# Shared expert ahead of the output projection, and the denominators' inverse ahead of clips, ranks and softplus chain

## The reference

```python
mod = (_silu(c) @ wmod).reshape(8, 6, 1, -1)             # sa, ca, ga, sb, cb, gb; |ga|, |gb| kept >= 0.25
h = _layernorm(x) * (1 + ca) + sa
x = x + ga * attention(h, W_in, W_out)
h = _layernorm(x) * (1 + cb) + sb
x = x + gb * ffn(h, ...)
# attention: xq, xk = clip(q/4), clip(k/4); Chebyshev polynomials Tq, Tk of orders 0..5 (orders above have weight 0)
num = (Tq * beta * cumsum(Tk * v)).sum(order)            # running sums over the tokens
den = (Tq.sum(channel) * beta * cumsum(Tk.sum(channel))).sum(order)
out = (num / (den + 1e-7)) @ W_out.T
# ffn: one shared expert and 8 routed ones, hidden size 128, top 2 of sqrt(softplus(logits))
shared = silu(h @ sW1 + sb1) @ sW2 + sb2
routed = sum_e cf[:, e] * (silu(h @ rW1[e] + rb1[e]) @ rW2[e] + rb2[e])
```

## Time and profile before

| | |
|---|---|
| median of 3 runs | 915.92 us (915.1 to 918.37) |
| the profiled execution's own time | 915.11 us |
| its span | 913.4 us |
| TensorE busy | 847.7 us (93%) |
| VectorE busy | 798.7 us (87%) |
| ScalarE busy | 486.2 us (53%) |
| GpSimd busy | 275.1 us (30%) |
| mean granted TensorE clock | 0.968 of full speed |

### The profile page before, as it was taken

One profiled execution on the slowest core, in us unless ns is written; L12 is line 12 of the kernel. 1 busy time (PEld: TensorE's weight loads), 2 busy tenths in 40 slices (PEclk: granted clock), 3 DMA queues, 4 the chain that ended last, 5 costly groups with the idle time before them and its releaser, 6 DMA issues. The chain is left out here.

```text
span 913.4 us, 14235 instructions
## 1 busy us (share of the span) xinstructions
PE 847.7 (93%) x4377; PEld 645.8 (71%) x4377; DVE 798.7 (87%) x1363; ACT 486.2 (53%) x874; POOL 275.1 (30%) x351
## 2 busy tenths in 40 slices
PE   5784749999999999999999999999999999998998
PEld 5553437786868677886768676877768676866786
DVE  3897969999999989999899989999999999999432
ACT  4753446555656466565656466565656464441321
POOL 1021241423434241423333251523333240413120
PEclk9886859999999999999999999999999999999999
DMA  9022225354544435354534435363635344353431
GB/s 322 2 55 75 47 49 168 71 169 87 152 87 114 129 75 167 70 168 88 149 88 119 125 72 167 71 176 85 167 72 137 76 81 135 78 152 76 122 94 45
DMA packets 51580, 99.98 MB, mean 109 GB/s; under 512 B 5363, under 2 KB 34110, under 8 KB 49478
## 3 DMA queue, kind: packets, MB, share of 16 engines
q1 hardware_dynamic: 36356, 66.14, 22.0%
q0 software_dynamic: 14688, 32.51, 20.5%
q10 hardware_dynamic: 482, 0.74, 0.2%
HBM read 57.68 MB, written 17.06 MB: 82 GB/s over the span
## 5 line engine op out<-in xcount | busy, mean ns | idle before, releaser
L1577 PE MATMUL acc<-w,hid 128*128 128x256 f32 x1128 | 262.6, 380 | 0.3 <-DVE hid L1219 0.3
L1577 PEld LDWEIGHTS acc<-w,hid 128*128 128x128 f32 x1128 | 214.0, 190 | 34.5 <-DVE hid L1219 0.5
L848 ACT ACTIVATE hid<-ring,b1row 128x512 f32<-128x512 f32 x144 | 96.8, 682 | 165.9 <-PE ring L1458 164.5
L673 POOL DMA_DIRECT2D feat<-feat x47 | 42.6, 906 | 344.0 <-DVE feat L1066 210.4
L796 ACT ACTIVATE feat<-ring,bqkv 128x512 f32<-128x512 f32 x96 | 65.9, 687 | 87.4 <-PE ring L1458 87.4
L1219 DVE TENSOR_TENSOR hid<-hid,cfw 128x512 f32<-128x512 f32 x128 | 85.0, 675 | 29.3 <-ACT hid L848 22.0
L1458 PE MATMUL ring<-n2H,w1H 128*128 128x512 f32 x288 | 106.2, 450 | 0.0
L1045 DVE TENSOR_TENSOR_SCAN feat<-zero,carry,feat 128x512 f32<-128x512 f32 x80 | 97.2, 1267 | 0.0
L1045 DVE TENSOR_TENSOR_SCAN feat<-zero,feat 128x512 f32<-128x512 f32 x80 | 92.4, 1205 | 0.0
L1458 PE MATMUL ring<-n2H,w1L 128*128 128x512 f32 x288 | 91.0, 397 | 0.0
L1458 PE MATMUL ring<-n2L,w1H 128*128 128x512 f32 x288 | 91.0, 397 | 0.0
(11 more groups left out here) (169 smaller groups left out, 1397.9 us busy)
## 6 DMA issues: line engine op xcount, KB each, us to landing
feat<-feat POOLq DMA_DIRECT2D x47, 512.0 KB, 4.6
cfw<-cf_rows SPq DMA_DIRECT2D x16, 1280.0 KB, 7.6
xin<-in_L_attn_x SPq DMA_DIRECT2D x16, 512.0 KB, 9.5
feat<-inv_rows SPq DMA_DIRECT2D x32, 256.0 KB
cfw<-cf_rows SPq DMA_DIRECT2D x16, 512.0 KB, 3.6
out<-x SPq DMA_DIRECT2D x15, 512.0 KB, 8.6
out<-fin POOLq DMA_DIRECT2D x15, 512.0 KB, 5.8
cfw<-cf_rows SPq DMA_DIRECT2D x16, 256.0 KB, 4.6
```

What stands on the lines that cost most here:

```text
L673: g.dma_start(f(into), f(of), accum_op=ALU.add).then_inc(added[n], 16)
L848: a.activation(hid[:, e % NG], ring[bank][:, :], ACT.Silu, bias=b1row[:, e:e + 1]).then_inc(ring_copied, 1)
L1577: last = mm(acc[t // 2][:, t % 2], hid[:, e % NG, t * P:(t + 1) * P], w2[:, e], start=False, stop=(e == E), skip_group_check=True)
```

## The change

The work is the same but for two places of memory and one wait; its order changes on TensorE, VectorE and ScalarE. SyncE's and GpSimd's instructions stand in the same order as before.

1. TensorE: `begin`, new, stands ahead of `project_out`. It does for the chunk c-1 the first part of its expert work: `expert_up` of experts 0 and 1 and `expert_down` of expert 0, and then `combine_by_expert`, which stood behind `project_out`. The next step starts with expert 2. `expert_down` of expert 0 now starts the accumulators and waits until `output` of the chunk before has read them; `second_biases` adds to them.
2. TensorE, inside the step: the projections k0 and k1 stand ahead of the second norm's transposes, the experts' downs come later against the ups, and the sixth up and the fourth down stand behind `denominators` and no more ahead of it.
3. VectorE: the next chunk's second pair of `odd` and its first `weigh` stand behind `output` and ahead of `residual`, instead of behind the norm's `lows`; `lows` of the second norm stand behind the weighings of experts 1 and 2.
4. VectorE: `logit_parts` is cut in two. The maxima stay; the ranks (three instructions) go behind the denominators' products, and `invert` follows them directly, ahead of the clips, the weighing of expert 5 and `softplus`. The ranks' temporary is no more the tile `prod` but a part of `feat`.
5. ScalarE: the silus of experts 0 and 1 stand at a step's end, and expert 3's ahead of the second norm; the k copies ahead of `highs` of the second norm.
6. The steps at both ends follow: step 1, which has no expert work before, now holds `begin` for chunk 0; `last_attention_step`, `step_after_attention` and `last_step` are written out.

```diff
-        RING = ["e0", "e1", "e2", "k0", "k1", "q0", "q1", "e3", "e4", "e5", "v0", "v1", "e6", "e7", "e8"]
+        RING = ["e2", "e3", "k0", "k1", "q0", "q1", "e4", "e5", "v0", "v1", "e6", "e7", "e8", "e0", "e1"]
...
-                pool.wait_ge(squares, 6 * c + 6)
+                pool.wait_ge(weighted, (ND - 1) * c + 1)
                 g.tensor_tensor(f(W + 4), f(KT5), f(V0), ALU.mult).then_inc(weighted5, 1)
...
@@ scalar step
                 if qkv:
                     highs(0, *nxt)
+                silu(2)
+                silu(3)
                 if second:
                     for t in range(NT):
                         normalise_second(act, *prev, t)
...
+                copy("k0")
+                copy("k1")
                 if second:
                     highs(1, *prev)
...
+                if st["begin"]:
                     for e in range(2):
-                        hidden(*prev, after, e)
+                        hidden(*prev, use, e)
...
@@ vector step
                     if attn_:
-                        odd(i, p, 1)
-                        weigh(i, p, 0)
                         weigh(i, p, 1)
+                        prefix(i, p, 0)
+                    expert(1)
+                    expert(2)
                     if second:
                         lows(1, *prev)
...
                 if second:
-                    logit_parts(*prev)
+                    logit_maxima(*prev)
                 if attn_:
                     den_key_sums(i, p)
                     den_products(i, p)
+                if second:
+                    logit_ranks(*prev)
+                if attn_ and not first:
+                    invert(i, p)
                 if qkv:
                     clip(*nxt, use, 0)
                     clip(*nxt, use, 1)
...
                 if ffn:
                     (last_output if is_last(*exp) else output)(*exp)
-                if qkv and not first:
-                    odd(*nxt, 0)
+                if qkv:
+                    if not first:
+                        odd(*nxt, 0)
+                    odd(*nxt, 1)
+                    weigh(*nxt, 0)
...
@@ tensor
+            def begin(i, p, use, st):
+                prev = later(i, p, -1)
+                if st["begin"]:
...
+                    expert_up(*prev, use, 0)
+                    expert_up(*prev, use, 1)
+                    expert_down(*prev, use, 0)
+                    if st is not AFTER_LAST:
+                        combine_by_expert(*prev, True)
```

243 lines of the change are left out of this document (133 added, 110 removed).

## The result

The changed kernel is slower. Its median is 925.36 us (920.96 to 926.73, 6 runs), against 915.62 us (915.1 to 921.14, 6 runs) for the kernel before. The ratio of the two sets of runs is 1.008, with a 95% interval of 1.0058 to 1.0103 (the medians alone would give 1.0106). The forecast was 906 us.

The account below looks back on a forecast made before the run. TensorE's own pace was taken to bound nine tenths of the program, at 50.43 us a full step. Terms -4.9, -1.8, -2.8 and 0 summed to -9.5 from 915.1: 905.6, as a median 906 us, range 902 to 910.

Parts of the forecast that it names:

- Step 1: End of step 1: inverse leaves 1.7 us earlier, projection runs at a better clock; -1.8 us, between 0 and -3.
- `begin` -4.9: Expert work ahead of the output projection fills step 1's wait of 12.83 us; all later work is 4.9 us less.
- last attention step and tail 0: After the full steps: remaining denominators' wait and later waits about equal the earlier losses; 0, between -3 and +3 us.
- Steps 2 to 14: Steady steps: inverse waits go, small denominators' waits come; 661.8 against 664.5 us, -2.8, bounds -8.9 and +6.5.
- Edits that cost nothing: Ranks' other tile, GpSimd's fifth-order product and routing weights, leaving 4 us earlier with first use as much earlier: no cost.
- The carry: ScalarE's carry copy, p = 0: VectorE waits 1.1 us instead of 0.77, giving a denominators' wait of 0.6.
- D: Rival: VectorE becomes the bound from T, the output projection's end, to `denominators`; 1.1 us in every step, 921 us; chance 0.07.
- B: Rival: cover is full, the 0.15 and 0.6 us waits in steady steps do not arise; 900 us; chance 0.18.
- C: Rival: the wait moves to low halves, transposes or denominators, 0.5 us a step more than counted; 912 us; chance 0.15.
- S: Rival: VectorE's clips lose 0.65 us a step to GpSimd's DMA issue, 9.1 us in 14 steps; 915 us; chance 0.05.
- E: Rival: the inverse's DMAs run into accumulating ones, division waits as now; under 2 us; counted with the forecast, together 0.55.
- The last sign: A wait at `denominators` of over 1 us in steps with p = 0 would show the prediction wrong as a whole.

Follow-up runs that it names:

- the three edits: Changed kernel with first spread bringing experts 1 and 2's weights, GpSimd's scaling kept off the first running sums, ScalarE's carry copy ahead of two scalings: 906.34 us, ratio 0.9891.
- the last one: Changed kernel with the three edits, and in `begin` the routing weights' transposes ahead of expert 0's down: 904.0 us, ratio 0.9849 to the kernel before.
- the edit W: Changed kernel, first of two DMAs spreading the routing weights carries experts 1 and 2 instead of one expert: 915.28 us, ratio 0.9983 to the kernel before.
- the run of the first half alone: Changed kernel with ranks again ahead of the denominators' products and the inverse behind the softplus chain: 939.08 us, ratio 1.0217 to the kernel before.
- S: Changed kernel, GpSimd's scaling of the output weights waits for the second norm's first high half, away from the first running sums: alone 926.93 us, ratio 1.0119.
- C: Changed kernel, ScalarE's carry copy stands ahead of its two scalings of the even orders: alone 917.37 us, ratio 1.0002 to the kernel before.
- the run on the kernel before: Kernel before, GpSimd's scaling of the output weights waits for the second norm's low halves, so it runs beside VectorE's first running sums: 920.15 us, ratio 1.001.

## Why the prediction was wrong, step by step

- *Step 1.* Forecast -1.8 us for the end of step 1. Measured 133.36 - 77.03 = 56.33 us from projection to T before, and 128.86 - 74.67 = 54.19 after: -2.1. The wait was split as forecast, its second part at the down of expert 0; it was 7.99 us and not under 7. Right, a little small.
- *`begin` -4.9, last attention step and tail 0.* The first term's gain can only show after the last full step: two ups less in the last attention step, a down less behind it. The two terms together said -4.9, measured -0.5. The last attention step waits 2.47 us for expert 1's hidden values (810.76), weighed late since VectorE waited for the weights, and 1.94 us for `output` (849.02). With the three edits it was -1.5 and with the last one, by which the routing weights leave earlier, -4.5: the work saved was real, and waits ate it, of which those for the routing weights were the larger part as far as these two single executions show. The term put at 0 for the last attention step and the tail failed by 4.4 us.
- *Steps 2 to 14.* Forecast -2.8, measured +10.9. The step that failed is the paragraph "Edits that cost nothing", on which this term rests. It said of the routing weights that they "leave 4 us earlier against the projection, while their first use comes as much earlier". Their write did leave 3.7 us earlier, but it took up to 1.6 us longer, so that the spreading DMAs started only 2.1 us earlier in step 6, and the use came 4.1 us earlier with p = 0 and 5.2 with p = 1. That is a wait of 0.22 to 1.40 us in 11 of the 13 steps, put at nothing in the forecast; the edit W took it away, and so did the earlier end of the write in the run of the first half alone. The same paragraph looked at GpSimd's fifth-order product but not at the scaling of the output weights, whose new neighbour is a pair of running sums: 1.1 us of VectorE's in steps with p = 0. The carry, which the forecast did see, was sized 1.1 us. It measured 0.69 behind the two other losses and 1.12 with both of them mended, which is the case that the forecast had reckoned with. The rest is small: the statistics start 1.11 us after T and not 0.8, as the forecast had it (the earlier trace rows gave 0.98).
- *What was right in it.* The sums of own times over 30 us: 27.83 - 0.82 = 27.0 us from the statistics to the products, 21.52 from the denominators to T against 21.6; no wait at the projection; the inverse's wait gone. With W, S and C the 13 steps took 787.39 - 127.43 = 660.0 us from projection to projection, where 661.8 was forecast, and the time is 0.9891 of before, 905.6 on that scale. That this meets the 905.6 of the sum is partly luck: the last part gave 1.5 us where the two terms had 4.9, the steps 4.5 where 2.8 was forecast, and step 1 2.6 instead of 1.8.
- *The rivals.* D had it: "VectorE becomes the bound in T to `denominators`", from 1.1 us in every step, of both p; measured 13.7/13 = 1.05 over the forecast. Its condition was "a waiting of VectorE that I do not see", and of that there were two. Its example, the second low halves coming late, came true in step 6 (0.92 us at `route_logits`). I gave it 0.07 because I had looked for waits among the things that moved, and not among those whose *user* moved. B was not so; C had the place (a cover too short) at half the size. S named the clips and GpSimd; the loss to GpSimd came true, but at the running sums; the clips themselves took 1.2 us in step 6. E was wrong: the inverse did come earlier.
- *The signs asked for.* "A mean step above 51.3 us would make the third term wrong": 51.95. The denominators wait of "half a us in every second step and none between" was 0.81 and 0.24. The last sign, a wait there of over 1 us with p = 0, did not show although the term failed: TensorE took part of the loss earlier, at `route_logits`.

## What to carry to other kernels

When an edit shortens the cover in front of a wait by nearly all its reserve, list each outside arrival that the uncovered engine still takes in (every DMA by the part of the data it brings, every copy by another engine, every instruction of GpSimd that may now meet VectorE's), with the distance to its *own* first use in the new order. For a DMA reckon with the time when it lands and not only when it leaves: here the write left 3.7 us earlier and ended only 2.1 us earlier, since it now ran closer behind another. Where several waits lie in a chain, mending one alone can measure as nothing, or as more than its size; mend them cumulatively and look at the next wait after each. And an early producer is worth having only where its input is there as early: the second half of the change (ranks and inverse) cost 3.5% alone, and on top of the first half it was worth 1.4% (1.0217 - 1.008).

## What the runs showed of the hardware

- VectorE and GpSimd did not share but took turns, a whole instruction at a time, and each one's record includes its waiting. Step 6 after: the scaling is issued at 340.74, just behind VectorE's product of 340.66; if it waits for that product's end at 341.8 and then takes its 1.29, it ends at 343.1, and its record says 340.74 + 2.29 = 343.03. The running sums, issued at 341.79, then begin at 343.0, and with 2.33 us end at 345.4; their record says 345.22. In the run on the kernel before it is the other way about: the scaling (353.81) waits for the first sum of the pair, which takes 1.2, then runs to 353.81 + 2.05 = 355.86; the second sum follows and ends at 353.55 + 3.39 = 356.94. So a collision costs VectorE up to about the GpSimd instruction's own time, once (1.10 us here, of 1.29), at whichever place they meet. The Trainium skill, "SBUF — State Buffer", section "SBUF: two separate sides", calls it an exclusive lock for the whole instruction; the trace agrees, with these numbers. The prediction had weighed the rule at the clips and not here. The division of step 0 is a third case: VectorE's timeline before, when it stood beside a product of GpSimd's of 2.72 us, and after, when that product came 4.5 us later:

```profile
73.54 3.43 DVE L1138 TENSOR_TENSOR feat<-feat 128x512 f32<-128x512 f32 x2
```

```profile
73.33 1.29 DVE L1138 TENSOR_TENSOR feat<-feat 128x512 f32<-128x512 f32 x2
```

- The write of 16 KB to DRAM, on which the spreading DMAs wait, took longer where it followed GpSimd's 512 KB write of the output by less. In step 2, where there is no such write yet, it took 1.45 us before and after. In steps 3 to 14 it was issued 2.5 to 3.0 us behind the output's before the change, and took 2.9 to 3.6 us; after, 1.8 to 2.2 us behind, and took 4.0 to 4.55. In both it ended 5.8 to 6.7 us after the issue of the output's write, which itself needs 5.8 us before and 6.2 after to land (medians of the page, part 6). It is not so when the write comes still closer: in five steps of the run with the transposes first it followed by only 0.8 us and took 1.5 to 1.7. No run moved one of the two writes alone, so the cause is read from these rows and not tried.
- Kernels whose programs are alike up to there reach step 0's projection at about 74.7, 76.8 or 78.9 us after the span's start. It is a matter of the single execution; of a difference under 4 us between two profiles the start has to be taken off first. What makes it was not looked for.
